# Another order of loads, splits and tasks before slot 8, and GpSimd's extra work by halves

## The reference, cut to what matters

```python
x = x + xattn(layernorm(x), ctx, ctx, proj_q, bias_q, proj_k, bias_k, proj_v, bias_v, w_out)
x = x + ffn(layernorm(x), w_gate, w_up, w_down)
# xattn: 16 heads, softmax(q k^T / 8) v, then hid @ w_out.T
# ffn: every linear layer quantises its input and its weights in blocks of 16
#      to the eight magnitudes of fp4, with one scale for a block;
#      h = silu(gate) * up, y = h @ w_down.T
```

## Time and profile before

| | |
|---|---|
| median of three runs | 397.33 us (394.61 to 397.7) |
| the profiled execution | 398.0 us |
| its span in the trace | 396.1 us |
| first score (slot 0) | at 32.04 us |
| score of slot 11 | at 75.31 us |
| eight slots in the middle (145.93 to 169.88) | 23.95 us |
| busy over the span | PE 84%, DVE 78%, ACT 67%, POOL 65% |

### The profile page before, as it was taken

One profiled execution on the slowest core, in us unless ns is written; L12 is line 12 of the kernel. 1 busy time (PEld: TensorE's weight loads), 2 busy tenths in 40 slices (PEclk: granted clock), 3 DMA queues, 4 the chain that ended last, 5 costly groups with the idle time before them and its releaser, 6 DMA issues.

```text
span 396.1 us, 9486 instructions
## 1 busy us (share of the span) xinstructions
PE 333.8 (84%) x3571; PEld 254.4 (64%) x3571; DVE 310.3 (78%) x629; ACT 266.7 (67%) x634; POOL 257.6 (65%) x254
## 2 busy tenths in 40 slices
PE   1777669998799989989895877898878999999976
PEld 1455448776587767767674666676656767677854
DVE  1979845766777778687899877679999999998692
ACT  3566687987899999999986689734352553542431
POOL 7272244786579898998985586738844667767510
PEclk9989958999999999999999899999998999999999
DMA  7990535797599899997995698831000000000001
GB/s 209 321 357 2 102 66 107 120 148 136 96 133 174 151 171 180 156 186 146 187 168 96 120 159 131 133 63 26 15 14 15 13 15 27 14 13 29 16 26 40
DMA packets 131710, 42.42 MB, mean 107 GB/s; under 512 B 123788, under 2 KB 129616, under 8 KB 131665
## 3 DMA queue, kind: packets, MB, share of 16 engines
q1 hardware_dynamic: 131665, 41.82, 55.3%
HBM read 8.78 MB, written 2.10 MB: 27 GB/s over the span
## 4 chain that ended last, share of the span: by engine, by line
DVE 42%; PE 32%; ACT 11%; issue 8%; POOL 4%; DMA 2%; SPq 0%; ACTq 0%; DVEq 0%
PE ps L572 5%; PE ps L493 5%; PE ps L495 5%; PE ps L494 5%; DVE arena L1191 4%; ACT arena L853 4%; DVE negmax L1110 4%; PE ps L629 4%; DVE arena L1141 3%; DVE arena L1193 3%; DVE arena L1314 3%; DVE arena L1280 2%; POOL arena L1387 2%; DVE arena L1126 2%; DVE arena L1145 2%
## 5 line engine op out<-in xcount | busy, mean ns | idle before, releaser
L1387 POOL TENSOR_TENSOR arena<-arena 128x640 f16<-128x640 f32 x64 | 93.0, 1453 | 58.0 <-ACT arena L863 57.6
L853 ACT ACTIVATE arena<-ps,negmax 128x154 f32<-128x154 f32 x256 | 78.6, 398 | 15.6 <-DVE negmax L1110 15.3
L572 PE MATMUL ps<-v_h,pT 128*128 128x132 f16 (+1 forms) x640 | 52.8, 214 | 17.2 <-DVE q_odd L1102 8.8
L1110 DVE TENSOR_REDUCE negmax<-ps 128x4 f32<-128x616 f32 x64 | 50.9, 795 | 20.1 <-PE ps L629 19.8
L572 PEld LDWEIGHTS ps<-v_h,pT 128*128 128x128 f16 x640 | 38.9, 100 | 24.6 <-issue 22.9
L1392 POOL TENSOR_TENSOR arena<-arena 128x256 f16<-128x256 f32 x64 | 46.5, 728 | 8.0 <-ACT arena L870 8.0
L863 ACT ACTIVATE arena<-arena 128x640 f16<-128x640 f32 x64 | 47.4, 741 | 1.2
L493 PE MATMUL ps<-arena 128*128 128x256 f16 (+1 forms) x144 | 41.6, 289 | 7.4 <-DVE arena L1013 5.9
L493 PE MATMUL ps<-arena,xnT_even 128*128 128x352 f16 x128 | 40.1, 313 | 4.8 <-DVE xnT_even L1202 4.1
L494 PE MATMUL ps<-arena 128*128 128x256 f16 (+1 forms) x144 | 41.3, 287 | 0.0
L495 PE MATMUL ps<-arena 128*128 128x256 f16 (+1 forms) x144 | 41.2, 286 | 0.0
(11 more groups left out here) (163 smaller groups left out, 943.7 us busy)
## 6 DMA issues: line engine op xcount, KB each, us to landing
out_dram<-arena SPq DMA_DIRECT2D x16, 128.0 KB, 1.7
pT<-arena SPq DMA_TRANSPOSE x70, 4.2
xs<-in_x_dram SPq DMA_DIRECT2D x2, 512.0 KB, 7.3
arena<-in_L_xattn_w_out_dram SPq DMA_DIRECT2D x1, 1024.0 KB, 11.8
xs<-in_x_dram SPq DMA_DIRECT2D x2, 384.0 KB, 6.7
wffn<-in_L_ffn_w_down_dram SPq DMA_DIRECT2D x1, 704.0 KB, 9.3
wffn<-in_L_ffn_w_gate_dram SPq DMA_DIRECT2D x1, 640.0 KB, 7.7
wffn<-in_L_ffn_w_up_dram SPq DMA_DIRECT2D x1, 640.0 KB, 8.2
```

The lines of the kernel that those rows point to most:

```text
L572: last = pe.matmul(o[:, h0 * HB:h1 * HB], pT[:, n % RING_P, part * CHUNKS + c], v[:, b, j, at[0]:at[-1] + 1].rearrange("p m k -> p (m k)") ...
L853: last = act.activation(prob[:, j, k * LP:k * LP + L], ps[:, 2 * (j % 2) + k % 2, (k // 2) * L:(k // 2 + 1) * L], ACT.Exp, bias=negmax[:, ...
L1110: dve.tensor_reduce(negmax[:, s, 4 * j:4 * j + 4].rearrange("p (k u) -> p u k", k=2), v, AX.X, ALU.max, negate=True).then_inc(max_done, 1)
L1387: pool.tensor_tensor(part_of(j, 1), prob[:, j], part_of(j, 0), ALU.subtract).then_inc(p_low, 1)
```

## The change

Loads: the x rows of steps 0 and 1 are loaded together ahead of the value bias, and the v projection ahead of the rest of x, not behind it.

Start: the low part of the k projection is made by GpSimd, one half (c) at a time with a semaphore for each, ahead of those of q, and the value bias stands between q and v. TensorE does twelve transposes of the identity after those of the context, makes the first three key pairs by halves, two more, then the rows of step 0, then the last three key pairs, and only the first two query tasks before slot 0. The other two and the rows of step 1 go into slots 0 and 1, the values into slots 1 to 4, the queries of step 1 into slots 2 to 5 and the output weights into slots 5 to 8. ScalarE splits q right after the value bias. VectorE takes the layer norm of steps 0 and 1 together, and that of steps 2 to 7 in slots 3 and 4 instead of 1 and 2.

Slots 6 to 56: `rows_normal` of step 2 is a slot later. From step 3 on `rows_high` is a slot behind `rows_normal`, `rows_low` is done by halves in the two slots behind that, and `turn_rows` comes two slots later. GpSimd's scaled value is made by halves in m = 2 and 3, and the product with the scale by halves in m = 7 and m = 0 of the next eight. The clearing of the padding of wdT moves from slot 16 to slot 20.

```diff
+WARM = 12
+KEYS_FIRST = 3
+KEYS_NEXT = 5
...
-            return n if b == 0 else 11 + 2 * n
+            return 1 + n if b == 0 else 11 + 2 * n
...
-            return (4, 4, 5, 6)[n]
+            return 5 + n
...
-            return 3 if i == 1 else 5 if i == 2 else 8 * (i - 1) - 6
+            return 6 if i == 2 else 8 * (i - 1) - 6
+
+        def rows_split_at(i):
+            return rows_at(i) + (0 if i == 2 else 1)
+
+        def rows_low_at(i, s):
+            return rows_split_at(i) + (1 if i == 2 else 1 + s)
...
-            return 6 + p // 2 if i == 1 else 8 * (i - 1) + (2 if i == 2 else 1) + p
+            return p // 2 - 2 if i == 0 else 2 + p // 2 if i == 1 else 8 * (i - 1) + (2 if i == 2 else 1) + p
...
-            out = [t for i in range(1, STEPS) for t in query_tasks(i) if query_at(i, t[2]) == n]
-            out += [("x", 1)] if n == 5 else []
+            out = [t for i in range(STEPS) for t in query_tasks(i) if query_at(i, t[2]) == n]
+            out += [("x", 1)] if n == 0 else []
...
-                sp.dma_start(xs[:, v, 0], x[0, rows_of(0, v)]).then_inc(ld_x0, 16)
+                sp.dma_start(xs[:, v, 0:2], pairs_of_rows(0)[v, :, 0:2]).then_inc(ld_x0, 16)
...
             load_proj("q", proj_q, ld_q)
+            load_proj("v", proj_v, ld_v)
...
-            load_proj("v", proj_v, ld_v)
...
-                    if rows_at(i) == n: turn_rows(i)
+                    if rows_low_at(i, 1) == n + 1: turn_rows(i)
...
+            for _ in range(WARM):
+                pe.transpose(ps[:, PROJ_BANK, 0:P], ident[:, :], ident[:, :])
...
+            for c in range(KC):
+                pe.wait_ge(wk_split, c + 1)
+                for p in range(KEYS_FIRST):
...
+            for p in range(KEYS_FIRST, KEYS_NEXT):
+                keys_of(p)
             turn_x(0)
-            pe.wait_ge(w_low, 2)
-            for t in query_tasks(0):
+            for p in range(KEYS_NEXT, PAIRS):
+                keys_of(p)
+            pe.wait_ge(w_low, 1)
+            for t in FIRST_QUERIES:
                 query(0, t[2])
...
-                last = dve.scalar_tensor_tensor(heads_of(wk_l, c), by_chunk("k")[:, c], 1.0, heads_of(wk_h, c),
-                                                ALU.mult, ALU.subtract)
-            last.then_inc(w_low, 1)
...
-            for b in range(B):
-                row_stats(b, 0).then_inc(stats_done, 1)
-            dve.wait_ge(stats_done, B)
-            layernorm(0, 1, 0)
+            stats_of(0)
+            stats_of(1)
+            dve.wait_ge(stats_done, 2 * B)
+            layernorm(0, 2, 0)
             normalise_x(0)
...
+            for c in range(KC):
+                proj_low(0, "k", wk_h, wk_l, c).then_inc(wk_split, 1)
+            proj_low(1, "q", wq_h, wq_l, 0)
+            proj_low(1, "q", wq_h, wq_l, 1).then_inc(w_low, 1)
             pool.wait_ge(bv_high, 1)
             pool.tensor_tensor(bv_l, bv_raw, bv_h, ALU.subtract).then_inc(bv_low, 1)
...
-                if n == 16:
+                    for s in range(B):
+                        if rows_low_at(r, s) == n: rows_low(r, s)
+                if n == 20:
                     pool.wait_ge(task_mm, TASK_AT[VALUES[-1]] + 1)
...
-                    if m == 7:
-                        pool.wait_ge(wgrid, w + 1)
...
+                    if m == 2: weights_value(w, 0)
+                    if m == 3: weights_value(w, 1)
+                    if m == 7: weights_round(w, 0)
+                if m == 0 and 2 <= i <= W_STEPS + 1: weights_round(i - 2, 1)
```

More of the change, by code:

```diff
@@ L314, in tasks_of @@
             return out
-        TASKS = [("x", 0)] + query_tasks(0)
+        FIRST_QUERIES = [t for t in query_tasks(0) if query_at(0, t[2]) < 0]
+        TASKS = [("x", 0)] + FIRST_QUERIES
         for n in range(SLOTS):
@@ L514, in _, with keys, keys_of @@
                 last.then_inc(job_mm, 1)
-            pe.wait_ge(job_low, J_CTX + KC)
-            pe.wait_ge(w_low, 1)
-            for p in range(PAIRS):
+            for _ in range(WARM):
+                pe.transpose(ps[:, PROJ_BANK, 0:P], ident[:, :], ident[:, :])
+            def keys(p, c):
+                return three(bank(J_K + p)[:, 0:B * L], wk_h[:, c, p * P:(p + 1) * P], wk_l[:, c, p * P:(p + 1) * P],
+                             cT_h[:, c, :, 0:L], cT_l[:, c, :, 0:L], c == 0, c == KC - 1)
+            pe.wait_ge(job_low, J_CTX + KC)
+            for c in range(KC):
+                pe.wait_ge(wk_split, c + 1)
+                for p in range(KEYS_FIRST):
+                    if c == 0: free(J_K + p)
+                    last = keys(p, c)
+                    if c == KC - 1: last.then_inc(job_mm, 1)
+            def keys_of(p):
                 free(J_K + p)
                 for c in range(KC):
-                    last = three(bank(J_K + p)[:, 0:B * L], wk_h[:, c, p * P:(p + 1) * P],
-                                 wk_l[:, c, p * P:(p + 1) * P], cT_h[:, c, :, 0:L], cT_l[:, c, :, 0:L],
-                                 c == 0, c == KC - 1)
+                    last = keys(p, c)
                 last.then_inc(job_mm, 1)
@@ L666, in task @@
                     if t == VALUES[0]:
[L667 removed]
+                        pe.wait_ge(w_low, 2)
                         pe.wait_ge(bv_low, 1)
@@ L786, in keys_out @@
                                bias=biasT[:, PAIRS + p:PAIRS + p + 1]).then_inc(job_high, 1)
-            for p in range(PAIRS):
+            for p in range(KEYS_NEXT):
                 keys_out(p)
-                if p == 3:
-                    act.wait_ge(ld_q, 16)
-                    split_proj("q", wq_h, 1.0)
             def x_high(i):
@@ L844, in _ @@
             high(("x", 0))
+            for p in range(KEYS_NEXT, PAIRS):
+                keys_out(p)
             def exps(n):
@@ L935, in slot @@
                 if n == 63: magnitude_x(1)
+            act.wait_ge(ln_step, LN_ROWS)
+            rows_normal(1)
+            for t in FIRST_QUERIES:
+                high(t)
             act.wait_ge(w_scaled, 1)
-            split_part("v", wv_h, 1.0, 0)
-            high(("q", 0, 0))
-            split_part("v", wv_h, 1.0, 1)
-            for t in query_tasks(0)[1:]:
-                high(t)
+            split_proj("v", wv_h, 1.0)
             act.activation(unused[:, 0:1], biasT[:, 0:1], ACT.Exp)
@@ L1091, in scale_proj, with keys_low @@
                 dve.tensor_scalar(raw[name], raw[name], WS, None, ALU.mult).then_inc(w_scaled, 1)
-            for p in range(PAIRS):
+            def keys_low(p):
                 dve.wait_ge(job_high, J_K + p)
```

100 lines of the change are left out of this document (59 added, 41 removed).

## The result

The changed kernel takes 400.81 us (median of 12 runs, 398.75 to 404.62) against 397.33 (12 runs, 394.61 to 398.82): a ratio of 1.0105, interval 1.008 to 1.013 (the two medians by themselves give 1.009). It is slower by 1%; 395.7 was forecast, and the range ended at 399.5. The profiled execution took 398.75 us with a span of 397.0, the fastest of the twelve, so its trace shows less than the typical loss.

What follows compares the result with a forecast made beforehand. ScalarE bounds steady steps; no engine is full from first to twelfth score. Terms -0.9 (to the twelfth score), +0.5 (clock), -1.2 (halves) and 0 (clearing) gave -1.6 from 397.33: 395.7 us, own range 393.5 to 399, full range 388 to 399.5.

Steps and rivals of the forecast that it cites:

- The start: Up to the first query: layer norm waits for GpSimd, rows ready at 24.2 instead of 19.1, first query 5.3 us late.
- The first rival: At the start: layer norm runs free of GpSimd, first query 7.7 us earlier than forecast, 388.0 us in all; chance 0.24.
- From T0 to the twelfth score: First query to score(11): early slots slower, slots 6 to 10 faster, twelfth score about 74.4 against 75.31, -0.9 us.
- T0: Time of the first query in the changed kernel, forecast at 29.5 us (29.0 to 30.0).
- +0.5 for the clock: Ahead of the fourth query TensorE stands some 2 us; a lower clock behind it costs 0 to 1.7, taken as +0.5.
- The second rival: Slots 6 to 10: the half clock of 50 to 55 us comes back, +5 us, 401 (399.5 to 403); chance 0.09.
- The halves: From slot 10 on: GpSimd's blocks by halves save one 0.3 us hole in each of four steps, -1.2 (-3.0 to +1.0).
- The 0 for the transposes of the identity: At the start: the twelve warm-up transposes lie in time in which TensorE only waits for the split, and cost nothing.
- added waits: From slot 10 on: waits for second halves, each with about a slot, 3 us, of cover; without it 0.7 each.

Runs made afterwards that it cites:

- e3: Changed kernel with GpSimd's low parts of q held until the rows of step 0 are normalised: 392.90 us, ratio 0.9909.
- g4: Changed kernel with only the low part of the value bias held until the rows of step 0 are normalised: 398.15 us, ratio 1.0028.
- g3: Changed kernel without the twelve transposes of the identity: 396.90 us, ratio 0.9999.
- e1: Changed kernel with the halves, the later high part and the clearing put back, so only the new start stays: 402.64 us, ratio 1.0158.
- e4: Changed kernel with the rows of step 2 made one slot earlier: 395.67 us, ratio 0.9962.
- e2: Kernel before with only the halves, their later slots and the clearing in slot 20: 393.62 us, ratio 0.9924.
- f2: Kernel before with only GpSimd's product with the scale by halves: 396.76 us, ratio 1.0004.
- f4: Kernel before with only the scaled value by halves: 398.56 us, ratio 1.0013.
- f3: Kernel before with only the low rows by halves, with later slots for high part and transpose: 395.07 us, ratio 0.9960.
- f1: Changed kernel with low parts of q held until step 0's rows are normalised and step 2's rows one slot earlier: 386.81 us, ratio 0.9745.
- g1: Kernel f1 with scaled value and product whole again, only the low rows by halves: 386.91 us, ratio 0.9748.
- h2: Kernel f1 without the twelve transposes of the identity: 387.26 us, ratio 0.9744.

## Why the prediction was wrong

**The start** was right: rows ready at 23.6 (24.2), first query at 28.95 (29.5), 4.7 us late, by the waiting that I had read from the earlier trace rows. e3 and g4 show the cause. The first rival, a free layer norm, did not come; made by hand in e3 it was worth 7.9 us, close to the 7.7 of its price. It gave 392.9 and not 388.0 because the 395.7 that it is taken from was itself 5 us too low, by the step that follows.

**The step that failed is "From T0 to the twelfth score".** I had -0.9, and +0.5 for the clock; the trace has +4.0, with a T0 that is 0.5 early, so this stretch is 5.5 us longer than worked out. By its own marks: score(2) comes at T0 + 14.1, not 12.1, since the stretch behind the pause at 38.05 runs at half clock for 3.4 us (1.5 us by e3's slot 1, of which the +0.5 covers a third) and the fourth query starts 0.5 late; score(6) is 2.2 late, 0.2 of it new; the transpose is issued at T0 + 40.9, not 38.1, another 0.6; it lands after 5.4 us, where I had put 3.1 to 4.9 although reads up to 5.5 (seven of the eight traces that issue it in this slot have 5.2 to 5.6, g3 3.9); and the last query and the score behind it take 4.1 us, not 2.8, because half clock followed that pause of 3.7 us too (2.8 in e1, where it didn't). The sum is 2.0 + 0.2 + 0.6 + 1.4 + 1.3 = 5.5. The mechanisms were named, but the wait for the transpose was taken as the end of the chain and not as a new stall that can cost the clock behind it too. e4 shows its size: without that wait the twelfth score is at 74.35.

**The second rival** priced the right effect, the half clock, at the wrong place: slots 6 to 9 ran at full clock, and it came behind the two pauses, where TensorE had stood. In slot 10, the last that it named, it cost 1.3 to 1.5 us of the 5. Its sign, a low clock beyond 58 us, was seen (0.66 from 75 to 80), and its range, 399.5 to 403, holds the 400.81; that is luck, as its mechanism gave under a third of its price.

**The halves** had the right sign and the wrong size: -1.2 was put, with a bound of -3.0; the trace has -4.65, and e2 by itself 0.76% of the time, 3.0 us. The term was one hole of 0.3 us in each of four steps. From slot 23 to slot 48 the trace gains 2.6; eight slots from 32 to 40 are 0.8 shorter (23.12 for 23.95), by the product (0.44 alone) and the low rows (0.34 alone), which let VectorE's rounding start ahead of GpSimd. The other 2.0 lie in slots 48 to 55, where I had not looked: slots 48 to 53 are together 2.1 longer, and slot 54 is 4.0 shorter (3.28 us for 7.30). TensorE in slot 54 of the kernel before:

```profile
219.67 0.60 PE L572 MATMUL ps<-v_h,pT 128*128 128x66 f16 x5 [3.28 <-DVE q_odd L1102]
...
220.00:222.00 2.00, 2.00 (x18) 0.50 1.13 216
```

and in slots 52 and 54 with the change:

```profile
213.27 0.60 PE L599 MATMUL ps<-v_h,pT 128*128 128x66 f16 x5 [2.61 <-DVE q_odd L1133]
...
214.00:216.00 2.00, 2.00 (x17) 0.50 1.09 206
...
220.63 0.40 PE L599 MATMUL ps<-v_h,pT 128*128 128x66 f16 x5 [0.47 <-DVE q_odd L1133]
```

Before, TensorE stands 2.61 us in slot 52, with full clock behind it, and 3.28 in slot 54, with half clock behind it. With the change the second pause is 0.47, and the half clock comes behind the first. e2, f2 and f4 have the short second pause too (0.38 to 0.47); f3 shortens the first instead. So each of the three pairs by itself changes these two slots. The 0 for the transposes of the identity holds for the first query; their effect on the median is open.

**The whole.** In the traced execution the lag comes to +4.0 at the twelfth score, +0.3 more by slot 23, -4.65 by slot 56 and +1.2 behind it: 0.9 us of span, where -1.6 was put. Of the 1.2, 0.5 is slot 57, where the weight transposes now wait for the second half of the product, one of the added waits that the prediction had named. The halves gained 3.4 us more than was put, and so hid as much of the error ahead of the twelfth score: that the forecast is 5.1 us off and not some 8.5 is luck. The traced execution, 398.75, would lie inside the range; the 2.1 us from there to the median lie in executions that were not traced.

## What to carry to other kernels

A move to an idle engine is priced by whom it holds, not by that engine's idle time: four operations of VectorE's chain of tiny ones were held 2 us each by GpSimd's operations of 2.1 us. Keeping three of these away with one wait, until the chain was through, gave the chain 5.6 us and took 2% off the time.

When a new order makes a late transfer the last thing to arrive, price the pause and the stretch behind it; one slot earlier was worth 5 us here. And look at every stretch with a different order of its own: here slots 48 to 55 moved 2 us.

Where two engines meet in a lock, look at which one starts first: a small operation put ahead turned it here, once in each of four steps.

## What the runs showed of the hardware that was not expected

A pause of TensorE of the same length, for the same wait, is followed by half clock in some executions and not in others: 2.38 us and 1.00 behind it, 2.37 us and 0.66; 3.50 us and 1.00, 3.72 us and 0.66. Single traces with the same start therefore differ by 1.5 us at such a place.

The same transpose of step 2's rows landed 3.9 us after its issue in g3 and 5.4 in the changed kernel, and the same start gave both. Issued a slot earlier (e4, f1, g1, h2) it landed after 3.3 to 3.6.
